# Attention: the block scores and reciprocals move from PSUM to SBUF, and two exponentials change places

## The reference: what is computed

```python
q, k = rope(q), rope(k)
k_cmp, v_cmp = block means of k and v over 64 rows
p_cmp = softmax(where(cmp_mask, q @ k_cmp * scale, -1e30)) * any(cmp_mask)   # block scores
o_cmp = p_cmp @ v_cmp
slc_mask = blk_sel & causal           # 8 blocks selected of 512 / 64 = 8: causal
o_slc = softmax(where(slc_mask, s_full)) @ v
o_swa = softmax(where(swa_mask, s_full)) @ v     # the last 64 rows
o = o_cmp * g_cmp + o_slc * g_slc + o_swa * g_swa
x = x + o @ Wo
```

## Time and profile before

| | |
|---|---|
| median of 3 runs | 2395.95 us (2394.24 to 2398.45) |
| profiled execution, span | 2393.1 us |
| PE busy | 2314.5 us, 97% of the span |
| DVE, ACT, POOL busy | 1850.5, 1491.4, 1620.9 us |
| mean granted clock of PE | 0.989 |

### The profile page before, as it was taken

How to read it: one execution, slowest core, us unless ns; L and a number is a source line. 1 busy time by engine, 2 the same in 40 slices (tenths; PEclk the granted TensorE clock), 3 DMA queues, 4 the chain that set the end, 5 groups by cost and what they waited for, 6 DMA issues and landing times. The chain is left out here.

```text
span 2393.1 us, 42078 instructions
## 1 busy us (share of the span) xinstructions
PE 2314.5 (97%) x13200; PEld 2037.1 (85%) x13200; DVE 1850.5 (77%) x6087; ACT 1491.4 (62%) x4161; POOL 1620.9 (68%) x1262
## 2 busy tenths in 40 slices
PE   6999999999999999999999999999987999999998
PEld 5799899989988898999899889888976788887787
DVE  8589898988888888989898888888882565566521
ACT  6577777777777777777777777777773111113343
POOL 2677877787787778778877877777763344444554
PEclk9999999999999999999999999999998999999999
DMA  5222222222232223222222322222225354453332
GB/s 172 74 61 60 75 74 60 69 78 63 54 86 63 66 55 91 58 64 74 73 58 63 86 61 60 67 73 54 67 80 186 130 197 145 162 177 118 113 121 79
DMA packets 143600, 213.32 MB, mean 89 GB/s; under 512 B 15008, under 2 KB 53280, under 8 KB 143392
## 3 DMA queue, kind: packets, MB, share of 16 engines
q1 hardware_dynamic: 137248, 196.17, 27.8%
q10 hardware_dynamic: 4224, 8.39, 0.9%
q0 software_dynamic: 1920, 6.24, 0.8%
HBM read 90.47 MB, written 53.22 MB: 60 GB/s over the span
## 5 line engine op out<-in xcount | busy, mean ns | idle before, releaser
L580 POOL TENSOR_TENSOR s_full<-s_full,rope 128x512 f32<-128x512 f32 x256 | 334.0, 1305 | 341.3 <-DMA s_swap<-s_full 341.1
L584 POOL TENSOR_TENSOR s_full<-s_full,s_swap 128x512 f32<-128x512 f32 x256 | 330.9, 1293 | 36.7
L581 POOL TENSOR_TENSOR s_swap<-s_swap,rope 128x512 f32<-128x512 f32 x256 | 330.7, 1292 | 0.0
L588 POOL TENSOR_TENSOR qk_lo<-s_full,qk_hi 128x512 fp32r<-128x512 f32 x256 | 326.5, 1294 | 0.0
L743 ACT ACTIVATE pt_hi<-bank 128x384 fp32r<-128x384 f32 (+1 forms) x384 | 174.8, 528 | 222.0 <-PE bank L682 221.6
L638 PE MATMUL bank<-wv_hi,xt_hi 128*128 128x256 f32 x1024 | 300.4, 293 | 0.0
L1040 POOL TENSOR_TENSOR o_lo<-o_raw,o_hi 128x2048 fp32r<-128x2048 f32 x32 | 147.2, 4601 | 221.4 <-ACT o_hi L1197 181.6
L749 ACT ACTIVATE bank<-bank,shift 128x512 f32<-128x512 f32 (+3 forms) x512 | 257.1, 502 | 60.1 <-DVE bank L854 59.7
L638 PE MATMUL bank<-wv_hi,xt_lo 128*128 128x256 f32 x1024 | 290.1, 283 | 0.0
L638 PE MATMUL bank<-wv_lo,xt_hi 128*128 128x256 f32 x1024 | 289.9, 283 | 0.0
L854 DVE TENSOR_REDUCE bank<-bank 128x8 f32<-128x512 f32 (+3 forms) x512 | 253.1, 494 | 0.0
(11 more groups left out here) (187 smaller groups left out, 6896.2 us busy)
## 6 DMA issues: line engine op xcount, KB each, us to landing
s_swap<-s_full SPq DMA_DIRECT2D x512, 128.0 KB, 2.3
o_scratch<-s_swap SPq DMA_DIRECT2D x128, 256.0 KB, 2.0
o_raw<-o_scratch SPq DMA_DIRECT2D x32, 1024.0 KB, 5.3
w_raw<-in_L_ffn_W SPq DMA_DIRECT2D x64, 256.0 KB, 3.0
xin<-in_L_attn_x SPq DMA_DIRECT2D x14, 1024.0 KB, 5.5
z_scratch<-z ACTq DMA_DIRECT2D x8, 1024.0 KB, 4.3
out<-x SPq DMA_DIRECT2D x32, 256.0 KB, 2.1
wq_raw<-in_L_attn_Wq SPq DMA_DIRECT2D x16, 256.0 KB, 3.0
```

The lines of the kernel that those rows point to most:

```text
L580: nc.gpsimd.tensor_tensor(s_full[k][:], s_full[k][:], rope[:, 0, :], ALU.mult).then_inc(cos_done[k], 1)
L581: nc.gpsimd.tensor_tensor(s_swap[k][:], s_swap[k][:], rope[:, 1, :], ALU.mult).then_inc(sin_done[k], 1)
L584: nc.gpsimd.tensor_tensor(s_full[k][:], s_full[k][:], s_swap[k][:], ALU.add).then_inc(roped[k], 1)
L588: nc.gpsimd.tensor_tensor(qk_lo[k][:], s_full[k][:], f32(qk_hi[k][:]), ALU.subtract).then_inc(lo_done[k], 1)
```

## The change

`sc` and `rc` become tiles of their own in SBUF, 32 and 12 numbers per partition, and ScalarE takes row tile 0's exponential before it waits for the block scores. The operations themselves, their number and their shapes stay as they are; L854's output, and the operands of L916 to L941 and L808 that were `sc` or `rc`, now lie in SBUF.

```diff
     cb = r("cb", [P, T, NB])
+    sc_sb = r("sc_sb", [P, T, NB])
+    rc = r("rc", [P, 3, T])
     assert r.at <= nc.sbuf_usable_end, (r.at, nc.sbuf_usable_end)
     o_sb = s_swap[1]
-    sc_at, rc_at = 256, 256 + T * NB
-    sc = banks[0][:, sc_at:sc_at + T * NB].rearrange("p (t n) -> p t n", n=NB)
-    rc = banks[0][:, rc_at:rc_at + 3 * T].rearrange("p (r t) -> p r t", t=T)
+    sc = sc_sb[:]
...
                     exp_of_row(u, 1)
                     exp_of_window(u, 1)
+                    exp_of_row(u, 0)
                     act.wait_ge(cmp_step, (u - 1) * NC + 3)
                     nc.scalar.activation(sc, sc, ACT.Exp).then_inc(exp_cmp, 1)
-                    exp_of_row(u, 0)
                     exp_of_window(u, 0)
```

## The result

The changed kernel takes 2551.79 us (median of 5 runs, 2550.68 to 2553.64) against 2395.95 us before (5 runs beside them, 2393.74 to 2398.45): 1.0653 times as long, 95% interval 1.0641 to 1.0665, some 156 us slower. The profiled execution has a span of 2548.9 us against 2393.1. The forecast was 2617 us with a range from 2490 to 2670; rival 1 (GpSimd lets VectorE in after each operation) had 2533 us.

What follows compares the result with a forecast made beforehand. PE was taken to bound the loop at 13.26 us a unit. Span 2393.1 + 190 (126 units at 1.51) + 31 (weight units) = 2614, with 2.9 from span to median 2617 us; range 2490 to 2670.

Steps and rivals of the forecast that it cites:

- rival 1: Attention loop: GpSimd lets VectorE in after each operation, nothing extra in weight units; 1.09 us a unit, 2533 us, chance 0.26.
- the second L588 behind L738: Sign in the profile after: GpSimd's second L588 starts after ACT's high part L738, released at about 7.1 us.
- and where GpSimd has its next operation ready, for that one too: VectorE operations with two SBUF inputs wait through GpSimd's queued work: L916 late by 2.34 us, L941 by 2.83.
- the order: Row tile 0's exponential ahead of the block scores' on ACT: takes 0.37 us off VectorE's chain; alone 3 to 8 us.
- the slack at PE's row tile 2: Tile 2's probabilities are ready at 8.23, PE reaches that tile at 9.19: about 1.0 us to spare.
- The forecast's walk: One unit traced with L916 and L941 held: PE's row tile 2 starts 1.68 us later, at 10.87.
- its settling: GpSimd's L584 settles 0.19 us ahead of L916, cutting the steady excess from 1.68 by 0.17 to 1.51 us a unit.
- Weight units: Last two units of seven groups: L941 also held by the weights' L164 and L160, 31 us, bounds 0 and 56.
- The row that I had costed at nothing: PE's clock: a wait of 1.5 us in 14.8 costs nothing, with 20 us as the upper end.
- 2 (only part is caught): L916 does not wait, later ones fall between GpSimd's operations: 25 to 50 us, some 2435 us, chance 0.07.
- 3 (no hold): Small VectorE operations are not held, PE stays the bound, only the turned order counts: about 2391 us, chance 0.08.
- 4 (L934 caught in place of L941): L934 falls behind the second L588: another 0.43 us a unit, 54 us more, 2671 us, chance 0.11.

## Why the prediction was right, and where it was not

**Sign, place and most of the size** came from three readings that held: PE was full and the chain of VectorE had something under one microsecond to give; the operations themselves cost the same in either place; and the change put five small operations in GpSimd's way. Most signs named in advance are there: unit 14.39 (14.3 to 14.9 foretold), DVE more busy, L941 near 1 us, L930 and L937 as before, PE's scores waiting for L888 (158 us, but 108.6 without the weight loads), the second L588 behind L738, L928's wait for L749 gone. Only L916, with 0.79 us, fell short of the 1 to 2.5 foretold, and POOL is not less busy but as busy, in a smaller share of a longer span.

**The step that failed is "and where GpSimd has its next operation ready, for that one too".** L916 was to be held through L584 and the first L588; it is held for what is left of L584, and L922 for what is left of L588. I had generalized the longest case, L1644, over the shorter ones, L1380 and L1362, in the same rows. Rival 1 is what happened; its 2533 us missed the median by 19 us, the forecast by 65. That the forecast came so near in spite of this step is in part luck, as the next sum shows.

**How the holds become time** can now be summed. For each kernel: the means of L916, L922, L932, L934 and L941 less those of the operations that aren't held (0.20, 0.20, 0.17, 0.19 and 0.15 us), added up, beside the median unit.

| kernel | holds, us a unit | unit less 13.26 | holds less the unit's growth |
|---|---|---|---|
| only rc in SBUF (old order) | 0.89 | 0.13 | 0.76 |
| after, old order | 2.26 | 1.48 | 0.78 |
| after | 2.29 | 1.13 | 1.16 |
| after, GpSimd in halves | 1.43 | 0.36 | 1.07 |
| after, rc in PSUM | 1.11 | 0.00 | at least 1.11 |

Two constants account for all five to within 0.05 us: the chain bears 0.77 us with the old order and about 1.12 with the new one, so the order is worth 0.35 (0.37 was foretold).

What the chain bears is mostly VectorE's own idle time, and not the slack at PE's row tile 2 from which the forecast read it. In the plain unit before, VectorE stands idle for 13.26 - 11.89 = 1.37 us: 0.71 at L928, 0.21 at L872, and 0.24 where it waits for PE's scores:

```profile
1009.39 0.50 DVE L859 TENSOR_TENSOR bank<-bank,causal 128x128 f32<-128x128 f32 x2 [0.24 <-PE bank L668]
```

In the unit of 14.32 us after, it stands idle for 0.56 us, 0.35 of it at L928 (1032.42), with no other wait of over 0.15 us. So VectorE's round now sets the plain unit, and PE waits for it. Over the 60 units in the middle of the groups the idle time falls by 0.88 us a unit, and VectorE's operations that are not held add up to 0.26 us less, above all L859, L864 and L872, which now overlap more with the operation ahead of them: together 1.14 us, the allowance of the table.

The forecast's walk had 2.83 + 0.37 - 0.17 = 3.03 us of holds and let 1.15 of the lateness pass unpaid (2.83 - 1.68) beside the order's 0.37, where the runs show 2.29 and 0.77. (The 0.17 was its settling, for which its own offsets give 0.19 - 0.01 = 0.18.) The holds were 0.74 too long, the allowance 0.38 too large, and part of the one error hid in the other: that is luck. The same holds for rival 1: its walk gives 2.61 us of holds, 0.32 too many, and its 1.09 us a unit comes near the 1.13 because the allowance is wrong by about as much, which is luck again. GpSimd's string also settled elsewhere: L584 starts 0.50 us ahead of L916 in the unit shown (1015.11 and 1015.61) and 0.61 in the median, not 0.19.

**Weight units.** Foretold: 31 us, from L941 held by L164 and L160 too. It got in ahead of L164 in the unit shown, and in the whole loop only three L941 were held by these two, for one operation each. Yet these periods lose more than the others: 56.1 - 28 x 1.13 - 7.9 = 16.6 us. The row that I had costed at nothing has a part in it: 1.0 us after PE's wait of 1.78 us the granted clock falls, and it reads 0.64, 0.50 and 0.73 in the stretches that follow, 0.50 being 1.2 GHz of 2.4; the transposes in that unit (L682, at 1008.98) take 2.33 us in place of the 1.25 of a plain one. After the 0.63 us of idleness in the plain unit it stays at 1.00. Over the loop there are seven such stretches at the weight loads, together 34 us at 0.50, and none there before; half of that, 17 us, is an estimate of the most that the clock can have cost. How the 16.6 us divide between the waits themselves and the clock no run here separates.

**Rivals.** 2 (only part is caught) fell: L916, a scalar_tensor_tensor, is held like the rest. 3 (no hold) fell as a forecast, but its gain is real: 2386.0 us where nothing is held. 4 (L934 caught in place of L941) does occur, in 8 units of 128. In four of them the L941 behind it is then free, as at 1034.96, and no second hold is paid; in the other four it is held as well, three times behind the weights' L160 or L164 (1.98 us at 1471.09).

## What to carry to other kernels

Before a tiny VectorE operand moves from PSUM to SBUF, count its SBUF inputs: with two, the operation waited here for the GpSimd tensor_tensor that was running, so its price is the rest of a GpSimd instruction (up to 1.3 us for 512 columns, more for 1024) and not its own 0.15 us; one operand left in PSUM takes the price away, and shorter GpSimd instructions took away two thirds of it (52 us lost in place of 156). Sum such holds along the chain and compare them with its slack before adding up edits: 38 us and 25 us, each alone, became 156 together (the 25 with the old order). Where a trace shows one long case and several shorter ones of a wait, weigh the shorter ones too.

## What the runs showed of the hardware that was not expected

- The hold goes both ways: where VectorE's L160 had started first, GpSimd's L580 took 1.56 us in place of its 1.29 (at 1008.26 after; in the kernel before 13 times, 1.41 to 1.66 us).
- In the attention loop one operation ahead is the rule, but in the last stage five of 32 L1644 let one to three further L1519 pass, before and after alike (1.9 to 4.3 us each). In the loop only requests made in the last moments of a GpSimd operation were passed over: after, one L916 asked 26 ns before L584's end and took 1.32 us; with GpSimd in halves, 21 did.
- Operands in SBUF made VectorE's unheld operations only 6 to 8 ns shorter: L928 186 ns against 192 from PSUM, L930 203 against 211. The Trainium skill, "VectorE: DVE Perf Modes", section on the TRN2 errata, has a fixed part 62 cycles smaller for SBUF sources, an estimate of 65 ns by its clock; the rows decide against it for operations this small. For ScalarE the exponential of 128x32 took 0.23 us in SBUF (the mean of 128) and 0.18 in PSUM.
